# Four graph passes in which TensorE picks 4 of every 32 source tiles that GpSimd gathered

## The reference

```python
# L0, four steps:
m = (h @ W_msg.T + b_msg).reshape(n, 4, 128)
r = segment_sum(m[src, edge_type], dst)
h = gru(r, h)
# L1, once:   msg = relu(attr2 @ w1) @ w2 * x[src] + x[src];  sum by dst, divide by count, linear, batch norm
# L2, once:   msg = h[src] @ W.T + b + emb[edge_type9];       sum by dst, GRU
# L3, once:   attention: k[src], v[src], q[dst], softmax over the edges of one dst, sum by dst, feed-forward
```

## Time and profile before

| | value |
|---|---|
| median of 3 runs | 5234.55 us (5216.54 to 5239.27) |
| profiled execution, and its span | 5233.15 us, 5231.4 us |
| mean granted TensorE clock | 0.665 |
| PE busy | 2481.9 us, 47% |
| POOL busy | 2834.5 us, 54% |
| DVE, ACT busy | 1519.5 us (29%), 424.8 us (8%) |
| chain that ended last | unknown queue or core 17%, PE 13%, DVE 10%, issue 7% |

### The profile page before, as it was taken

How to read it: one execution, slowest core, us unless ns; L and a number is a source line. 1 busy time by engine, 2 the same in 40 slices (tenths; PEclk the granted TensorE clock), 3 DMA queues, 4 the chain that set the end, 5 groups by cost and what they waited for, 6 DMA issues and landing times.

```text
span 5231.4 us, 42580 instructions
## 1 busy us (share of the span) xinstructions
PE 2481.9 (47%) x12006; PEld 2039.6 (39%) x12007; DVE 1519.5 (29%) x3455; ACT 424.8 (8%) x692; POOL 2834.5 (54%) x2944
## 2 busy tenths in 40 slices
PE   5223363233522336444466656652333655555387
PEld 3222232222322333443345555532322445544374
DVE  3111141111411114222242222211111555555874
ACT  1000010000100001000010000110000100000133
POOL 3666636666466664666635665346666355554000
PEclk8556575555755567555567887865566766666699
DMA  4111121111211112111111111111111233333140
GB/s 158 47 44 47 45 76 47 46 45 44 77 47 46 45 44 78 46 45 46 44 31 40 42 42 39 27 41 45 47 46 42 68 114 121 121 121 106 49 148 25
DMA packets 146356, 318.40 MB, mean 61 GB/s; under 512 B 51123, under 2 KB 65658, under 8 KB 145786
## 3 DMA queue, kind: packets, MB, share of 16 engines
q0 software_dynamic: 99840, 218.29, 15.9%
q1 hardware_dynamic: 46458, 99.48, 5.4%
HBM read 255.94 MB, written 61.63 MB: 61 GB/s over the span
## 4 chain that ended last, share of the span: by engine, by line
another core or an unknown queue 17%; PE 13%; DVE 10%; issue 7%; DVEq 1%; POOL 1%; ACT 1%; DMA 0%; ACTq 0%
PE ps L1266 12%; DVE oh L815 2%; DVE small L1065 1%; DVE ring L1055 1%; DVE ring L1062 1%; DVE ring L983 1%; DVE pw L1056 1%; POOL ring L431 0%; DVEq L815 0%; POOL small L441 0%; PE ps L1380 0%; DVE ring L1097 0%; DVE ring L1144 0%; DVE nodes L1098 0%
## 5 line engine op out<-in xcount | busy, mean ns | idle before, releaser
L431 POOL DMA_INDIRECT ring<-m_tab,idx x1664 | 1606.8, 966 | 1003.2 <-issue 487.5
L1266 PE MATMUL ps<-oh,ring 128*128 128x128 f32 x5824 | 1236.9, 388 | 1906.5 <-DVE oh L815 1082.3
L1266 PEld LDWEIGHTS ps<-oh,ring 128*128 128x128 f32 x5824 | 1129.0, 286 | 1987.1 <-issue 1963.5
L815 DVE TENSOR_TENSOR oh<-cst,dl 128x256 f32<-128x256 f32 x1664 | 591.6, 419 | 2582.5 <-remote 2146.8
L431 POOL DMA_INDIRECT ring<-x_tab,idx x832 | 797.3, 958 | 462.3 <-issue 237.0
L431 POOL DMA_INDIRECT ring<-kv_tab,idx x416 | 399.2, 960 | 288.8 <-DVE rec L1070 147.4
L441 POOL TENSOR_TENSOR small<-small,bc 128x4 f32<-128x4 f32 (+1 forms) x28 | 31.0, 1109 | 635.9 <-DVE small L906 635.9
L1266 PE MATMUL ps<-wpad,rts 128*128 128x128 f32 x832 | 180.8, 360 | 261.0 <-issue 191.8
L1266 PEld LDWEIGHTS ps<-wpad,rts 128*128 128x128 f32 x832 | 149.1, 256 | 292.9 <-issue 220.3
L1266 PE MATMUL ps<-nodes,wt 128*128 128x512 f32 (+1 forms) x532 | 237.6, 588 | 36.1 <-DVE nodes L840 11.2
L494 ACT ACTIVATE nodes<-ps 128x512 f32<-128x512 f32 x18 | 9.4, 597 | 2924.5 <-PE ps L1266 2924.5
(11 more groups left out here) (233 smaller groups left out, 1999.3 us busy)
## 6 DMA issues: line engine op xcount, KB each, us to landing
ring<-m_tab,idx POOLq DMA_INDIRECT x1664
ve_dr<-pw SPq DMA_DIRECT2D x52, 512.0 KB
ring<-ve_dr SPq DMA_DIRECT2D x52, 512.0 KB, 3.4
m_tab<-ring SPq DMA_DIRECT2D x75, 256.0 KB, 2.1
ring<-x_tab,idx POOLq DMA_INDIRECT x832
ring<-kv_tab,idx POOLq DMA_INDIRECT x416
m_tab<-oh SPq DMA_DIRECT2D x25, 256.0 KB, 2.1
nodes<-in_xT SPq DMA_DIRECT2D x2, 1600.0 KB, 10.3
```

What stands on the lines that cost most here:

```text
L431: pool.indirect_dma_start(ring[:, u, j, 0:width], None, table, bass.IndirectOffsetOnAxis(ap=idx[:, g * WV + j:g * WV + j + 1], axis=0)).th ...
L815: ins = V.tensor_tensor(oh[:, v, j:j + 2, :], iota.unsqueeze(1).to_broadcast([P, 2, P]), dl[:, ds((i * RING + (u + ahead)) * WV + j, 2)].u ...
L1266: return T.matmul(o, lhsT, rhs, start=start, stop=stop, skip_group_check=True)
```

## The change

In the passes k = 0, 1, 2 and in L2, POOL leaves out the last four slots of the fourth wave of each turn (slots 28 to 31 of 32). PE fills these four places of the ring itself:

1. *Split.* At the start of such a pass the nodes (h in L0, x in L2) are turned by PE, and ACT and DVE split each f32 value into three bf16 parts whose sum is exact. These `pieces` (25 windows x 3 x 128) lie in the memory of `recT`.
2. *Select.* Each turn SP brings the source numbers of the 512 edges, one row spread to 128 partitions (256 KB, into the memory of `wpad`). For each of 25 node windows a selector of 128x512 in bf16 is made: one where the source number is the node's. DVE makes 10 of them with one comparison each, ACT 15 with two operations each (a square of the difference, then relu(1 - d)). They share five buffers.
3. *Pick.* PE multiplies for each window the three parts with the selector, 75 bf16 matmuls of 512 columns into PSUM bank 7: windows 0 to 8 behind the turn's first wave, 9 to 24 behind the second. ACT copies the sum out (`pickT`).
4. *Turn.* In L0 each of the four picked blocks is multiplied with the message weights of all four types plus the bias (`turned_by_type`), before places 0, 2, 4 and 6 of the third wave; DVE masks by edge type and adds the four up into the ring. In L2 PE only transposes (`turned`), and one DVE copy follows. PE waits for that before place 4 of the fourth wave.

Since `recT` and `wpad` are overwritten, `recT` is stored to DRAM first (ACT's `hidden` of the first pass waits for this), and both are loaded again before L1 and before L3. The source numbers are also stored to DRAM once, and DVE gets some 20 small operations before the first pass.

The diff, cut to its core:

```diff
 def gathers(k, table, width, idx):
...
-                    for j in range(WV):
+                    for j in range(WV - GS if selects(k) and u == RING - 1 else WV):
...
+            sp.wait_ge(s_ac, AC[f"recT{WAVES // 4 - 1}"])
+            sp.dma_start(recT_dr, recT[:, :]).then_inc(g_spill, 16)
+            def src_rows(r):
+                with sp.Fori(0, TURNS) as i:
+                    sp.wait_ge(g_used, (r * TURNS + i) * WIN + AHEAD)
+                    row = src_dr[ds(i * (RING * WV) + G_FROM, GS), :].rearrange("(a s) e -> a (s e)", a=1)
+                    sp.dma_start(src_row, row.to_broadcast([P, GS * P])).then_inc(g_row, 16)
+            def restore(r):
+                sp.wait_ge(g_used, r * (TURNS * WIN) + AHEAD)
+                sp.dma_start(recT[:, :], recT_dr).then_inc(g_back, 16)
+                sp.dma_start(wpad_f, a["wpad"]).then_inc(g_back, 16)
...
+            def selectors(g, i):
+                for n, w_ in enumerate(BY_AC):
+                    b = n % 2
+                    if n == 0:
+                        act.wait_ge(g_row, (g * TURNS + i + 1) * 16)
+                    nc.scalar.activation(dist[:, b, :], src_row, ACT.Square,
+                                         bias=node_m[:, w_:w_ + 1]).then_inc(g_dist, 1)
+                    act.wait_ge(g_dist, (g * TURNS + i) * len(BY_AC) + (n + 1))
+                    act.wait_ge(g_used, (g * TURNS + i) * WIN + (w_ - SBUFS + 1 + AHEAD))
+                    nc.scalar.activation(sel[:, w_ % SBUFS, :], dist[:, b, :], ACT.Relu, scale=-1.0,
+                                         bias=ones[:, 0:1]).then_inc(g_sa, 1)
+                act.wait_ge(g_used, (g * TURNS + i + 1) * WIN + AHEAD)
+                nc.scalar.activation(pickT, ps[:, 7, :], ACT.Copy).then_inc(g_pick, 1)
...
+            act.wait_ge(g_spill, 16)
...
+            def selectors(g, i, ws):
...
+                        dve.wait_ge(g_used, (g * TURNS + i) * WIN + (w_ - SBUFS + 1 + AHEAD))
+                        V.tensor_scalar(sel[:, w_ % SBUFS, :], src_row, node_p[:, w_:w_ + 1], None,
+                                        ALU.is_equal).then_inc(g_sv, 1)
+            def picked_by_type(g, i):
+                for j in range(GS):
+                    n = (g * TURNS + i) * GS + j
+                    dve.wait_ge(g_tr, n + 1)
+                    dve.wait_ge(g_slot, n + GS)
+                    V.tensor_tensor(typed.rearrange("p (t d) -> p t d", d=D),
+                                    ps[:, 7, :].rearrange("p (t d) -> p t d", d=D),
+                                    maskG[:, ds(i * GS + j, 1), :].rearrange("p a t -> p (a t)").unsqueeze(2)
+                                    .to_broadcast([P, ET, D]), ALU.mult).then_inc(g_typed, 1)
+                    dve.wait_ge(g_typed, n + 1)
+                    V.tensor_reduce(ring[:, RING - 1, WV - GS + j, 0:D], typed.rearrange("p (t d) -> p d t", d=D),
+                                    AX.X, ALU.add).then_inc(g_slot, 1)
+            def sums_by_two(k, g, pick):
+                split_nodes(g)
+                with dve.Fori(0, TURNS) as i:
+                    for u in range(RING):
+                        dve.wait_ge(credit, wave_no(k, i, u) + 3)
+                        one_hot(k, i, u).then_inc(oh_ready, 1)
+                        if u == 0:
+                            selectors(g, i, G_PARTS[0])
+                        if u == 1:
+                            selectors(g, i, [*G_PARTS[1], *G_PARTS[2]])
+                    pick(g, i)
...
+            def split_nodes(g, h):
+                for c, (c0, cw) in enumerate(CH):
+                    for j in range(cw // P):
+                        ins = T.transpose(ps[:, c, j * P:(j + 1) * P], h[:, c0 + j * P:c0 + (j + 1) * P], ident)
+                    ins.then_inc(tb_mm, 1)
+                pe.wait_ge(tb_r1, (g + 1) * NCH)
+            def pick(g, i, ws):
+                for w_ in ws:
...
+                    pe.wait_ge(made, (g * TURNS + i) * len(by) + (by.index(w_) + 1))
+                    for k in range(PARTS):
+                        ins = mm(ps[:, 7, :], pieces[:, w_, k, :], sel[:, w_ % SBUFS, :], start=(w_ + k == 0),
+                                 stop=(w_ == WIN - 1 and k == PARTS - 1))
+                    ins.then_inc(g_used, 1)
+            def turned_by_type(g, i, j):
...
+                if j:
+                    pe.wait_ge(g_typed, n)
+                mm(ps[:, 7, :], pickT[:, j * P:(j + 1) * P], w("L0_WmsgT", 0, 4), stop=False)
+                mm(ps[:, 7, :], ones_b[0:PARTS, :], bias_b[0:PARTS, :], start=False).then_inc(g_tr, 1)
+            def sums_by_two(k, g, turn):
...
+                            if u == 2 and j % 2 == 0:
+                                if j == 0:
+                                    pe.wait_ge(g_pick, g * TURNS + i + 1)
+                                turn(g, i, j // 2)
+                            if u == RING - 1 and j == WV - GS:
+                                pe.wait_ge(g_slot, (g * TURNS + i + 2) * GS)
+                        if u == 0:
+                            pick(g, i, G_PARTS[0])
+                        if u == 1:
+                            pick(g, i, G_PARTS[1])
+                            pick(g, i, G_PARTS[2])
```

More of the change, by code:

```diff
@@ L60 @@
 MT_SLOTS = [len(range(b, WIN, RING)) for b in range(RING)]
+GS = 4
+G_FROM = RING * WV - GS
+GPASS = STEPS - 1
+SBUFS = 5
+AHEAD = 2 * WIN
+BY_DV = [w for w in range(WIN) if w % SBUFS in (1, 3)]
+BY_AC = [w for w in range(WIN) if w not in BY_DV]
+G_PARTS = [range(0, 9), range(9, 18), range(18, WIN)]
+PARTS = 3
 assert WAVES % RING == 0
@@ L85, with selects, landed @@
 PASS_L1, PASS_L2, PASS_L3 = STEPS, STEPS + 1, STEPS + 2
+def selects(k):
+    return k < GPASS or k == PASS_L2
+def landed(k, u, i):
+    if u < RING - 1:
+        return (k * TURNS + i + 1) * (16 * WV)
+    short = TURNS * 16 * (WV - GS)
+    full = TURNS * 16 * WV
+    before = {GPASS: GPASS * short, PASS_L1: GPASS * short + full, PASS_L2: GPASS * short + 2 * full,
+              PASS_L3: (GPASS + 1) * short + 2 * full}
+    if isinstance(k, int) and k >= GPASS:
+        return before[k] + (i + 1) * (16 * (WV - GS if k == PASS_L2 else WV))
+    return (k * TURNS + i + 1) * (16 * (WV - GS))
 class Any1(dict):
@@ L531, in norm @@
                                          ACT.Copy).then_inc(ln_o, 1)
+            act.wait_ge(g_spill, 16)
+            act.wait_ge(s_dv, DV["g_init"])
             with act.Fori(0, STEPS - 1) as s:
                 hidden(s, "L0")
+                split_nodes(s)
+                with act.Fori(0, TURNS) as i:
+                    selectors(s, i)
                 evac(s)
@@ L577, in _ @@
             hidden(STEPS, "L2")
+            split_nodes(GPASS)
+            with act.Fori(0, TURNS) as i:
+                selectors(GPASS, i)
             evac(PASS_L2)
@@ new lines, in picked @@
+            def picked(g, i):
+                dve.wait_ge(g_tr, (GPASS * TURNS + i) * GS + GS)
+                V.tensor_copy(ring[:, RING - 1, WV - GS:WV, 0:D],
+                              ps[:, 7, :].rearrange("p (s d) -> p s d", d=D)).then_inc(g_slot, GS)
+            def sums_by_two(k, g, pick):
[9 more added lines that the diff above has]
+                    pick(g, i)
@@ L1023, in _ @@
             dve.wait_ge(oh_ready, (PASS_L1 + 1) * WAVES + 1)
-            sums(PASS_L2)
+            sums_by_two(PASS_L2, GPASS, picked)
             evac(PASS_L2)
@@ L1326, in _ @@
             blocks = [(b * P, min(P, TILES - b * P)) for b in range(4)]
+            for b in range(-(-SLOTS // P)):
+                tn = min(P, SLOTS - b * P)
+                ins = T.transpose(ps[0:tn, 5, b * P:(b + 1) * P], rec[:, b * P:b * P + tn, F_SRC], ident)
+            step("srcT", ins)
             for b, (t0, tn) in enumerate(blocks):
@@ new lines, in sums_by_two @@
+            def sums_by_two(k, g, turn):
+                with pe.Fori(0, TURNS) as i:
+                    for u in range(RING):
+                        cs = load_cols(pe, cols, i, u)
+                        pe.wait_ge(gat[u], landed(k, u, i))
+                        pe.wait_ge(oh_ready, oh_no(k, i, u))
+                        for j in range(WV):
+                            if u == 2 and j % 2 == 0:
[4 more added lines that the diff above has]
+                                pe.wait_ge(g_slot, (g * TURNS + i + 2) * GS)
+                            ins = mm(psf[:, ds(cs[j], P)], ring[:, u, j, 0:D], oh[:, u % 2, j, :], start=False,
+                                     stop=False)
+                        ins.then_inc(credit, 1)
+                        if u == 0:
[3 more added lines that the diff above has]
+                            pick(g, i, G_PARTS[2])
@@ L1410, in after_recT @@
             def after_recT():
[L1411 removed]
+                pe.wait_ge(s_ac, AC["srcT"])
                 pe.wait_ge(s_dv, DV["t_d1"])
@@ L1502, in _ @@
             hidden(STEPS, "L2", xT)
+            split_nodes(GPASS, xT)
             zero(range(NCH))
-            sums(PASS_L2)
```

(1 more changed line is left out.)

150 lines of the change are left out of this document (140 added, 10 removed).

## The result

The changed kernel took 5593.2 us (median of 4 runs, 5584.7 to 5611.2) beside 5236.9 us for the kernel before on the same chip: a ratio of 1.0693, 95% interval 1.0654 to 1.0732. The forecast was 5010 us, with 4790 to 5340 as the range. It is 7% slower, and outside the range. The profiled execution took 5590.9 us (span 5589.1).

What follows compares the result with a forecast made beforehand. POOL's gather pace, then late credits, was taken to bound the kernel. PE's chain would take over at 40.5 us a turn; L0 passes -51, -51, -27 and L2 -95 sum to -224, from 5233 to 5010 us, range 4790 to 5340.

Steps and rivals of the forecast that it cites:

- The chain of a turn: Dependent work of PE, ACT and DVE in a changed L0 turn: 31.4 us at full clock, 26.6 of it matmuls.
- The typed products: Product by message weights plus bias in an L0 turn: 1.09 us each, 1.83 us when DVE's type mask must come first.
- The clock: PE's mean clock in the changed L0 turns: 0.87, stretching 26.6 us of matmuls to 30.6 us.
- The handoffs: Five PE signals to ACT or DVE on an L0 turn's chain, half of 1.61 us each: 4.0 us a turn.
- supply: ACT and DVE making selectors in five buffers, ACT barely keeping up with PE's picks: 1.2 us a turn added.
- The start of a pass: Splitting the nodes before zeroing delays PE's first wave from 722.56 to about 730, some 7.5 us.
- spill: Storing recT to DRAM before the first pass's `hidden`: 22 us, putting PE's first wave at about 105.
- L2: Pass without typed turns: POOL bounds it at 35.4 to 37.7 us a turn, 95 us gained.
- The restores: Loading recT and wpad again, 22 us and 7 us, hidden under L0's fourth pass and L2's update: no cost.
- POOL's 28 x 1.266 us: POOL's own gather pace in a changed turn: 28 gathers at 1.266 us, 35.4 us instead of 40.5.
- the forecast's own formula: Whole change as 39 T - 1803.5 us, T being the L0 turn; zero at T = 46.2.
- Rival (b): Each handoff of the turn loses what L1's do, clock 0.78: turn 48.1 us, kernel about 5340 us; chance 0.24.

Runs made afterwards that it cites:

- Experiment 1: A tiny matmul behind each wave in the kernel before (ratio 0.9989), and behind each picked window, typed product and wave in the changed kernel (1.0902).
- before_drained: Kernel before, with POOL waiting after each wave in three L0 passes until its gathers land; 4823.8 us beside 4574.0 on the fast chip.
- before_oh4: Kernel before with four one-hot buffers instead of two in three L0 passes and L2; ratio 1.0006.
- before_tail: Kernel before with one tiny matmul behind each wave's last product in the passes of L0 and L2; ratio 0.9989.
- before_drained_again: Kernel before, with POOL waiting after each wave in three L0 passes until its gathers land, on the slow kind of chip; 5290.5 us beside 5239.6.
- after_pauses_8: Changed kernel, POOL waiting for its gathers after waves 0, 1 and 3 of a turn in three L0 passes and L2, pauses in other passes too; ratio 1.0556.

## Why the prediction was wrong

**The chain of a turn: right in kind, 2.9 us short.** 31.4 us at full clock were forecast; 34.3 are measured at a clock of 0.99 without gathers in the way. The typed products are the main part: 2.42 us apart, not 1.83. The pair and the bias take 1.35 us, not 1.09, and DVE starts 0.2 us behind them (at 1107.96, the bias done at 1107.74), a handoff that the sum left out; the wave's two products (0.71) do lie under DVE's work, as forecast. The reduce took 1.04 us, not 0.7. Together that is 3 x 0.6 + 0.3 + 0.3 = 2.4 of the 2.9 us.

**The clock: nearly right.** 0.83 where 0.87 was taken, with PE busy 69% of the pass where 70 to 80% was forecast. (As a mean of levels of 0.5 and 1.0, 0.87 is 74% of the time at the high one.)

**The handoffs: the step that failed.** "PE works on beside most of them, so I take half: 5 x 0.8 = 4.0." The gathers cost the turn 51.0 - 34.3 = 16.7 us (4.0 of that was charged to the clock, 4.0 to handoffs, 1.2 to supply). On the fast chip, with all gathers and no late signal, a turn took 35.7, so some 15 us of it are the lateness. Two things were wrong in it. The count: five handoffs on the chain were priced, while the 25 signals by which PE gives selector buffers back were treated as supply for which five buffers were slack enough. They aren't, when a signal comes up to 19 us late. And the price: 1.61 us was taken from L1, as a mean over 208 operations. The rows of the pass itself had the right size in view: DVE at 752.62 waits for the pass's first wave, which ended at 724.61, so that signal was 28 us late, and the next one, of the wave that ended at 736.30, 31 us. They were put aside with the words that PE had nothing more to do then. Experiment 1 shows that this isn't the condition.

**The start of a pass.** 7.5 us for the split were forecast from its operations, 34 us came in the second pass, for the same reason: seven signals of PE, each waited for, with POOL gathering. In the first pass the same lateness was hidden by a spill of half the forecast length.

**L2.** "There POOL is the bound": its turn was 43.8 us, not 37.7, by the same late signals. Without typed turns it lost little against before instead of winning 95 us.

**Where it was right.** The restores and the other passes at nothing; POOL's 28 x 1.266 us; by luck, the start of the first pass. The turn at which nothing is won or lost was put at 46.2 us; with the longer starts it lies lower. With 51.0 in the forecast's own formula, 39 x 51.0 - 1803.5 = +186 us, and 2 x 27 us for the starts, 80 + 34 for L2 (6.1 x 13 us and its start) come to some +350; 358 were measured. Rival (b) had the nearest mechanism, handoffs that lose time, and the direction, with the wrong handoffs and too small a price (48.1 us). It was given 0.24.

**Shown and not shown.** Shown: the slowdown lies in the four passes; the chain without gathers in a row is short enough (34.3 us); on a chip where nothing is late two near relatives of the changed kernel are 2.6 to 2.8% faster than the kernel before (a third 0.9%); the lateness needs gathers in a row and ends when POOL pauses long enough. The changed kernel word for word wasn't run on that chip, so that it is faster there is likely, not shown. Not settled: why gathers in a row hold PE's signals up, why pauses that cure the kernel before don't cure the changed one, and what sets the fast chip apart, which was met in one group only. Whether the profiler has a part in the lateness isn't settled either: every execution here comes with a span and a clock that it read. That PE's instruction count between pauses decides is argued from four kernels, with one against it, and not tested by itself.

## What to carry to other kernels

When the trace shows signals that arrive long after the work, count every signal of that engine that a new loop waits for, those that only give buffers back too, and price each at what the same stretch shows, not at a mean from elsewhere. Taking work from a busy engine and giving it to one whose signals are late can make the late one the bound, and more buffers can just move the place where it shows. And look at the bound on more than one chip before calling a few per cent a property of the kernel.

## What the runs showed of the hardware

- Chips differ. The same kernel before took 5217 to 5242 us in most groups and 4574 in one, 12.7% less, with gathers at the same 1.25 us. before_drained ran on both kinds: 467 us apart, of which 434 lie in the stretches in which four passes gather without pauses (526.5 against 594.2 us in the counting pass, 524 against 701 in L1, 526 against 592 in L2, 525 against 649 in L3).
- On the first kind, with POOL gathering in a row, PE's signals came up to 31 us late in the kernel before and up to 19 us late in the changed one. In before_oh4 the pattern repeated every 40 gathers, 56.9 us apart, each time ending in a stall of POOL (6.5 to 6.8 us; 5.3 to 6.5 in before_tail). There PE's own issue fell to one instruction, weight load or matmul in turn, each 1.40 us.
- A pause of POOL of 1.8 us after every 8 gathers kept PE's signals within 0.2 us in the kernel before (before_drained_again). In after_pauses_8 pauses of 1.8 us left them up to 12 us late.
- Back-to-back tensor_scalar operations of DVE with f32 in and bf16 out stop a gather for as long as they last (2.62 instead of 0.94 us).
